# A four-layer graph network on one core: layer 3 in 34 shared tiles instead of 40, and a reordered passage from layer 1 to layer 2

## The reference

```python
# layer 2
Wh = h @ W
e = leaky_relu((Wh @ a1)[:, None] + (Wh @ a2)[None, :])
scores = where(adj > 0, e, -9e15)
x = x + elu(softmax(scores, axis=1) @ Wh)
# layer 3, for all pairs (i, j): a logarithmic map in the ball, masked, summed over j
u = mobius_add(-h_i, h_j);  un = clip(norm(u), 1e-7, 1 - 1e-5)
logs = 2 / lambda(h_i) * arctanh(un) * u / un
v_i = sum_j where(adj[i, j] > 0, logs[i, j], 0)
x = x + expmap(v, h)
```

## Time and profile before

| | |
|---|---|
| median of 3 runs | 1027.44 us (1025.52 to 1030.37) |
| the profiled execution's own time | 1028.51 us |
| its span in the trace | 1026.4 us (2.1 us lie around it) |
| busy share of the span | PE 89%, DVE 71%, ACT 55%, POOL 54% |
| chain that ended last | PE 73%, DVE 18%, issue 5%, ACT 3% |
| the layer 3 loop | 835.55 us to 994.57 us |
| passage from layer 1 to layer 2 | about 737 us to 762 us |

### The profile page before, as it was taken

The page is one execution under the profiler, slowest core; times in us unless marked ns, Lnnn a source line. Parts: engine busy times, 40 slices in busy tenths (PEclk is TensorE's granted clock), DMA queues, the critical chain, the costliest instruction groups (busy, mean ns, idle before and its releaser), DMA issues.

```text
span 1026.4 us, 17924 instructions
## 1 busy us (share of the span) xinstructions
PE 913.0 (89%) x6942; PEld 332.0 (32%) x6942; DVE 733.4 (71%) x1177; ACT 563.5 (55%) x977; POOL 556.2 (54%) x660
## 2 busy tenths in 40 slices
PE   6899999999999999999993798999769679999960
PEld 5733222222222222222232522333333244554420
DVE  4655568788888788887867477222549659999987
ACT  2688666666666666666650365001120248899960
POOL 2367569898898989898850000000000018899961
PEclk9689999999999999999995599999959867999985
DMA  8570211111112111110000000000000000000000
GB/s 173 139 141 17 62 61 38 59 40 64 40 32 65 35 70 40 60 38 26 23 12 0 1 1 1 1 1 2 1 1 1 1 0 1 1 0 1 1 0 21
DMA packets 22874, 32.62 MB, mean 32 GB/s; under 512 B 14427, under 2 KB 14555, under 8 KB 21766
## 3 DMA queue, kind: packets, MB, share of 16 engines
q1 hardware_dynamic: 20486, 23.10, 7.4%
q0 software_dynamic: 2304, 8.39, 4.4%
HBM read 38.58 MB, written 1.29 MB: 39 GB/s over the span
## 4 chain that ended last, share of the span: by engine, by line
PE 73%; DVE 18%; issue 5%; ACT 3%; SPq 0%; DMA 0%; POOL 0%; DVEq 0%; ACTq 0%
PE ps L1209 22%; PE ps L1219 11%; PE ps L1349 8%; PE ps L1196 6%; DVE big L453 5%; PE ps L1188 4%; PE ps L1374 3%; PE ps L1297 3%; PE ps L1410 2%; DVE big L785 2%; DVE big L450 2%; PE ps L1065 2%; PE ps L1287 2%; PE ps L1042 1%; PE ps L1382 1%
## 5 line engine op out<-in xcount | busy, mean ns | idle before, releaser
L587 DVE COPY_PREDICATED big<-mask,ps 128x512 f32<-128x512 uint8 x512 | 341.5, 729 | 113.6 <-PE ps L1196 109.9
L406 POOL TENSOR_SCALAR big<-big 128x512 f32<-128x512 f32 x512 | 355.7, 714 | 74.2 <-PE ps L1219 72.3
L933 ACT ACTIVATE ps<-ps 128x512 f32<-128x512 f32 x512 | 268.6, 583 | 141.6 <-PE ps L1188 141.3
L1209 PE MATMUL ps<-big 128*32 128x512 f32 x2048 | 253.6, 600 | 0.0
L422 POOL TENSOR_TENSOR big<-big 128x512 f32<-128x512 f32 x40 | 67.3, 1683 | 324.3 <-ACT big L1015 324.3
L1219 PE MATMUL ps<-big 128*32 128x512 f32 x1024 | 134.6, 597 | 0.0
L1188 PE MATMUL ps<-op_r,op_l 18*128 18x512 bf16 x512 | 111.7, 384 | 3.8 <-DVE big L587 2.2
L1209 PEld LDWEIGHTS ps<-big 128*32 128x32 f32 x2048 | 53.7, 109 | 119.7 <-issue 110.4
L1410 PE MATMUL ps<-big 66*128 66x512 f32 x160 | 86.2, 669 | 2.2 <-DVE big L758 1.3
L1196 PE MATMUL ps<-op_r,op_l 9*128 9x512 bf16 x512 | 74.7, 388 | 0.4 <-ACT ps L933 0.2
L453 DVE TENSOR_TENSOR big<-big,mask 128x512 f32<-128x512 f32 (+1 forms) x72 | 65.8, 933 | 12.7 <-ACT big L957 11.3
(11 more groups left out here) (258 smaller groups left out, 1153.9 us busy)
## 6 DMA issues: line engine op xcount, KB each, us to landing
big<-max_scratch SPq DMA_DIRECT2D x8, 1024.0 KB, 4.5
big<-rden_scratch SPq DMA_DIRECT2D x30, 256.0 KB, 3.3
big<-in_adj_dram POOLq DMA_DIRECT2D x12, 512.0 KB, 9.2
op_l<-split_scratch SPq DMA_DIRECT2D x56, 36.0 KB
op_r<-split_scratch SPq DMA_DIRECT2D x56, 36.0 KB
work<-in_adj_dram POOLq DMA_DIRECT2D x2, 512.0 KB, 12.9
h_nat<-in_adj_dram POOLq DMA_DIRECT2D x2, 512.0 KB, 11.8
x_nat<-in_x_dram SPq DMA_DIRECT2D x1, 512.0 KB, 5.1
```

What stands on the lines that cost most here:

```text
L406: pool.tensor_scalar(ring[:, k % RING, :], vrow[:, head % 2, i0:i0 + HALF], HUGE, g0[:, head, jt:jt + 1], ALU.min, ALU.max).then_inc(s["ba ...
L587: dve.copy_predicated(ring[:, k % RING, :], mask[:, jt, i0:i0 + HALF], ps[:, slot("tile", k), :])\
L933: act.activation(ps[:, at_slot, :], ps[:, at_slot, :], ACT.Relu, scale=-1.0).then_inc(s["relus"], 1)
L1209: m = pe.matmul(ps[32 * w:32 * (w + 1), MAIN, :], vp[:, head, jt + w // 2, 32 * (w % 2):32 * (w % 2 + 1)], ring[:, (u + w // 2) % RING, :] ...
```

## The change

It has two parts. In layer 3 a tile becomes a list of pieces. The strip on the diagonal of row `jt` keeps only the 128-blocks from the diagonal to the right (4, 3, 2 or 1 blocks for `jt % 4` = 0, 1, 2, 3), and short strips share a tile of 512 columns: 3 + 1 blocks of rows `jt-2` and `jt`, 2 + 2 blocks of rows `jt-4` and `jt`. All blocks off the diagonal are mirrored now, those inside the strips too, so all 34 tiles go through transposes and the mirror's mask product. Matmuls, the masked product and the mirror's mask product are issued once for each piece. In the passage from layer 1 to 2, PE's order is changed.

```diff
-        TILES3 = [(jt, c) for jt in range(NT) for c in range(jt // (HALF // P), BLOCKS)[::-1 if jt else 1]]
+        def diagonal(jt):
+            return (jt, jt // TB, jt % TB, TB)
+        TILES3 = [[diagonal(0)]] + [[(0, c, 0, TB)] for c in range(1, BLOCKS)]
+        for jt in range(1, NT):
+            TILES3 += [[(jt, c, 0, TB)] for c in range(BLOCKS - 1, jt // TB, -1)]
+            if jt % TB == 0:
+                TILES3.append([diagonal(jt)])
+            elif jt % TB == 3:
+                TILES3.append([diagonal(jt - 2), diagonal(jt)])
+            elif jt % (2 * TB) == TB + 2:
+                TILES3.append([diagonal(jt - TB), diagonal(jt)])
+        def pieces(k):
+            at = 0
+            for jt, c, b0, b1 in TILES3[k]:
+                yield at * P, jt, c, b0 * P, (b1 - b0) * P
+                at += b1 - b0
+        def mirrors(k):
+            for at, jt, c, i0, width in pieces(k):
+                skip = P if c == jt // TB else 0
+                if width > skip:
+                    yield at + skip, jt, c * TB + (i0 + skip) // P, (width - skip) // P
...
# DVE
-                if k >= LAG_M and MIRROR[k - LAG_M]:
+                if k >= LAG_M:
...
+                    dve.wait_ge(s["turned3"], m + 1)
+                    for at, jt, ib, blocks in mirrors(m):
+                        r = tt(wA[:, u, at:at + blocks * P].rearrange("p (j n) -> p j n", n=P),
+                               ps[:, 2, at:at + blocks * P].rearrange("p (j n) -> p j n", n=P),
+                               mask[:, ib:ib + blocks, jt * P:(jt + 1) * P], ALU.mult)
...
-                    tt(wC[:, u, :], wD[:, u, :], mask[:, jt, c * HALF:(c + 1) * HALF], ALU.mult).then_inc(s["wm3"], 1)
+                    for at, jt, c, i0, width in pieces(m):
+                        r = tt(wC[:, u, at:at + width], wD[:, u, at:at + width],
+                               mask[:, jt, c * HALF + i0:c * HALF + i0 + width], ALU.mult)
+                    r.then_inc(s["wm3"], 1)
...
# PE, layer 1 to 2
             turn_h(2)
             values2(1)
+            row_scores(0)
+            row_scores(1)
+            turn_h(3)
             values2(2)
-            for c in range(3):
-                row_scores(c)
-            turn_h(3)
             values2(3)
...
             pe.matmul(ps[:, 4, 3 * P - 1:3 * P], onesf[0:1, :], small[0:1, 20:21], start=True, stop=True).then_inc(s["mxb"], 1)
+            row_scores(2)
             row_scores(3)
...
# PE, layer 3: transposes and sums
+                    pe.wait_ge(s["wgt"], m + 1)
+                    if m >= 1:
+                        pe.wait_ge(s["mirrored"], m)
+                    for at, jt, ib, blocks in mirrors(m):
+                        for o in range(at, at + blocks * P, P):
+                            r = pe.transpose(ps[:, 2, o:o + P], wD[:, m % NW, o:o + P], ident[:, :])
...
+                    for n, (at, jt, c, i0, width) in enumerate(pieces(m)):
+                        pe.matmul(ps[0:DX, 4 + c, i0:i0 + width], h[:, jt, :], wC[:, u, at:at + width], start=(jt == 0),
+                                  stop=(FINAL[c] == (m, 0, n)))
+                    pe.wait_ge(s["mirrored"], m + 1)
```

More of the change, by code:

```diff
@@ L345, in gnn_stack @@
         n1 = len(TILES1)
-        TILES3 = [(jt, c) for jt in range(NT) for c in range(jt // (HALF // P), BLOCKS)[::-1 if jt else 1]]
-        n3 = len(TILES3)
-        MIRROR = [c > jt // (HALF // P) for jt, c in TILES3]
-        MIRRORS = [sum(MIRROR[:k + 1]) for k in range(n3)]
+        def diagonal(jt):
[9 more added lines that the diff above has]
+                TILES3.append([diagonal(jt - TB), diagonal(jt)])
+        n3 = len(TILES3)
+        def pieces(k):
[8 more added lines that the diff above has]
+                    yield at + skip, jt, c * TB + (i0 + skip) // P, (width - skip) // P
+        FINAL = {}
+        for k in range(n3):
+            for n, (at, jt, c, i0, width) in enumerate(pieces(k)):
+                FINAL[c] = (k, 0, n)
+            for n, (at, jt, ib, blocks) in enumerate(mirrors(k)):
+                FINAL[jt // TB] = (k, 1, n)
         LAG_T, LAG_M, LAG_S = 4, 5, 6
@@ L1409, in _ @@
                             pe.wait_ge(read, k)
-                        pe.matmul(ps[:, bank, :], lhs3[0:DX, jt * P:(jt + 1) * P], rhs[0:DX, c * HALF:(c + 1) * HALF],
-                                  start=True, stop=True).then_inc(sem, 1)
+                        for at, jt, c, i0, width in pieces(k):
+                            r = pe.matmul(ps[:, bank, at:at + width], lhs3[0:DX, jt * P:(jt + 1) * P],
+                                          rhs[0:DX, c * HALF + i0:c * HALF + i0 + width], start=True, stop=True)
+                        r.then_inc(sem, 1)
                 m = k - LAG_T
-                if 0 <= m < n3 and MIRROR[m]:
+                if 0 <= m < n3:
                     pe.wait_ge(s["wgt"], m + 1)
-                    if MIRRORS[m] > 1:
-                        pe.wait_ge(s["mirrored"], MIRRORS[m] - 1)
-                    for j in range(HALF // P):
-                        r = pe.transpose(ps[:, 2, j * P:(j + 1) * P], wD[:, m % NW, j * P:(j + 1) * P],
-                                         ident[:, :])
+                    if m >= 1:
[3 more added lines that the diff above has]
+                            r = pe.transpose(ps[:, 2, o:o + P], wD[:, m % NW, o:o + P], ident[:, :])
                     r.then_inc(s["turned3"], 1)
@@ L1422, in _ @@
                 if m >= 0:
-                    u, (jt, c) = m % NW, TILES3[m]
+                    u = m % NW
                     pe.wait_ge(s["wm3"], m + 1)
-                    r = pe.matmul(ps[0:DX, 4 + c, :], h[:, jt, :], wC[:, u, :], start=(jt == 0),
-                                  stop=(jt == (c + 1) * (HALF // P) - 1))
-                    if MIRROR[m]:
-                        pe.wait_ge(s["mirrored"], MIRRORS[m])
-                        for j in range(HALF // P):
-                            r = pe.matmul(ps[0:DX, 4 + jt * P // HALF, jt * P % HALF:jt * P % HALF + P],
-                                          h[:, c * (HALF // P) + j, :], wA[:, u, j * P:(j + 1) * P],
-                                          start=False, stop=False)
+                    for n, (at, jt, c, i0, width) in enumerate(pieces(m)):
+                        pe.matmul(ps[0:DX, 4 + c, i0:i0 + width], h[:, jt, :], wC[:, u, at:at + width], start=(jt == 0),
+                                  stop=(FINAL[c] == (m, 0, n)))
+                    pe.wait_ge(s["mirrored"], m + 1)
+                    for n, (at, jt, ib, blocks) in enumerate(mirrors(m)):
+                        for j in range(blocks):
+                            r = pe.matmul(ps[0:DX, 4 + jt // TB, jt % TB * P:jt % TB * P + P], h[:, ib + j, :],
+                                          wA[:, u, at + j * P:at + (j + 1) * P], start=False,
+                                          stop=(FINAL[jt // TB] == (m, 1, n) and j == blocks - 1))
                     r.then_inc(s["sums"], 1)
```

11 lines of the change are left out of this document (3 added, 8 removed).

## The result

The changed kernel takes 1011.33 us (median of 4 runs, 1009.67 to 1018.69) against 1026.48 us for the kernel before (4 runs, 1024.45 to 1030.37). The ratio is 0.9866, 95% interval 0.9837 to 0.9894: 1.3% faster. The ratio weighs all runs; the two medians alone would give 0.985, and the ratios further on weigh all runs in the same way. The forecast was 1009.0, in a range of 1000.5 to 1018.0.

A forecast was written before the change was run, and what follows sets the result against it. Layer 3 was taken as bound by DVE's turn and the DVE-POOL gate, both 3.6 to 3.7 us; the passage by PE. Passage -6.5 and layer 3 -12.0 take 1028.5 to 1010.0, less 1.1 to the median: 1009 us, range 1000.5 to 1018.

The forecast's parts named there:

- Step 1: Passage from layer 1 to 2: row products 0 and 1 ahead of the last transposes, 2 behind the maximum; -6.5 us.
- Step 2: Layer 3: 40 turns become 34; start +0.8 us, then 26 turns instead of 32 at 3.72 us, 96.7 us, less 0.6.
- Step 3: Layer 3, PE: fine on average, but whole tiles in a row make L779 lose the gate once; +1.3 us (0 to 2.6).
- Step 4: Layer 3: POOL enters between a split tile's two masked products, 1.4 us each, three tiles in the loop; +4.2 us.
- The rival without a stall: Split tiles in layer 3: DVE issues the second piece so tightly that POOL stays out; 1004 us, chance 0.20.
- Step 5: End of layer 3: 16 us from the last L785 to the end of the sums, +4.9 us; another +4 if the clock falls.
- Half clock or more lost gates: Layer 3: PE at half clock in the end, or more lost gates, +4 to +6 us; 1014 us, chance 0.20.
- The passage without gain: Passage from layer 1 to 2: ACT's table load or the row products become late, no gain; 1015.5 us, chance 0.04.
- the slower case: Layer 3: whole tiles in a row keep PE late, L779 loses to L426 nearly every turn; 1040 us, chance 0.03.

The follow-up runs named there:

- the kernel with every stall removed: Changed kernel with the six shared tiles' masks packed by ACT and ACT's exponential for tile k-2 moved ahead of tile k-1's exp and ln: 1006.20 us, ratio 0.9812.

## Why the prediction was right, and where it wasn't

**Step 1, the passage: right.** 6.5 us forecast, 6.6 in the trace, 6.5 alone in the time. The row products behind the maximum stayed hidden, as the comparison of PE's and ACT's start had it.

**Step 2, six turns fewer: right in the turn, short in the start.** The 20 turns of the loop without a stall average 3.70 us, so that 26 of them make 96.3 (96.1 forecast). But the start costs 2.15 us instead of 0.8. In the kernel before the clock rises 23.2 us after tile 0's L785, in the changed one 26.8, although transposes now begin one tile earlier. PE is at the half clock for 3.6 us longer, and DVE waits 2.60 us for it at 854.04. I had taken the clock's rise as fixed. The rise is at 26 to 27 us in all kernels with 34 tiles and at 23.2 in the one with only the passage changed, so it belongs to layer 3's part; what in PE's work moves it stays open.

**Step 3, PE: this step failed.** It said "on average PE is fine", since 127 us were less than the 134.5 of before. The comparison that counts is with DVE's time for the same turns: 127 / 34 = 3.74 us a turn against 3.70. And an average over all tiles is too kind, because part of the sums falls behind the last turn. In the 26 turns of the loop PE has 98.5 / 26 = 3.79 us a turn, as the kernel with every stall removed shows in 99.10 us. PE was short by 0.09 us a turn on average over the whole loop, not only in the first twelve tiles. (Before, 14 of the loop's 32 tiles had no mirror, more than the "every fourth tile or so" of the prediction, and PE was far from short.) Each time its lag reaches DVE's L481 the margin of 0.15 us is gone, L811 loses the gate, and 1.3 us are paid at once: three lost gates instead of one, +2.6 us.

The second slip is in what a lost gate gives back. The prediction had 1.1 us, enough for six turns of 0.17, so that one lost gate would do. But the traces have the next ones after four turns each (7, 11, 15). Timeline of PE over the first of these long turns, in the changed kernel:

```profile
860.75 1.88 PE L1446 MATMUL ps<-big 66*128 66x512 f32 x4
863.00 0.63 PE L1456 MATMUL ps<-ident,big 128*128 128x128 f32 x4 [0.37 <-DVE big L484]
...
865.20 1.88 PE L1446 MATMUL ps<-big 66*128 66x512 f32 x4
```

DVE's turn takes 5.01 us, but PE's takes 4.45 instead of 3.89, because its transposes wait for DVE's late mirror's mask product. So PE gains only 0.56 us, and in the fourth turn of 0.17 that is used up. A fourth gate would have been lost, had not the splits' stalls given PE its lead back: leaving out the masks of second pieces brought it out at turn 24.

**Step 4, the split masked products: right.** 1.4 us each forecast, 1.3 measured (5.01 against 3.70, and 1.32 in the kernel with all products split). The Trainium skill, "SBUF — State Buffer", section "Who interferes with whom", has the shared pair of ports as a lock for a whole instruction, taken in the order of issue. The traces agree: 1.83 us for two pieces with POOL waiting, 0.76 without. What a single row couldn't show and the split of all products does: between two instructions of DVE that follow each other directly, a waiting POOL gets in each time. The rival without a stall is refuted. One reading of the prediction was loose: L422 ends 1.13 us, not 1.27, behind the end of the masked product's record (871.07 against 869.94); counted from the product's start, as the gate's sum does, the 3.68 us stand.

**Step 5, the end: right in its size, with a wrong part.** 16 us forecast, 16.74 measured. The clock stayed at 1.00, as taken. The stall of tile 30 was foreseen, a second one was not: at 965.08 the masked product of tile 31, one instruction of 512 columns, loses against L457, issued 0.08 us earlier, and lasts 1.72 us. It is the same kind of loss by an 0.1 us margin.

Together: 1.35 at the start, 2.5 in the loop and 0.7 in the end are the 4.6 us by which layer 3 gave 7.4 instead of 12.0. Of these the loop's are shown by experiment (a kernel without lost gates and splits, one without splits), the start's only by the traces. The single profile hid them by starting layer 3 earlier for another reason.

**The rivals.** No stall at the split tiles (1004) is refuted. Half clock or more lost gates (1014) is half right: more gates were lost and the clock stayed up. With the start and the end they make up the 4.6 us of the traces, of which the medians show 3.3 (15.1 us gained, where the forecast had 18.4). The passage without gain and the slower case didn't come; the argument against the latter held in kind, a lost turn gives PE back what several turns use up, but four turns and not six.

**What beats it.** Packing the six masks brings the ratio to 0.983, with ACT's order also moved to 0.981 (of these two, the second is shown over the first by the trace alone: the medians are 1006.26 and 1006.20 us). Of a change that merges short pieces of work, that is the part that should have come with it: the pieces share a tile for every engine, but not for the one instruction that stands at the gate.

## What to carry to other kernels

Where instructions of two engines exclude each other, as DVE's with both inputs in SBUF and POOL's do here, count how many enter, not only how many elements they handle: one instruction split in two cost 1.3 us here against 0.07 of work, because the other engine was already waiting. When several engines are within 3% of one another, compare each one's total with the total of the engine that sets the pace, over the same turns, and not with its own total before; a shortage of 0.09 us a turn was paid in steps of 1.3 us. And when a profile's difference agrees with a sum, look first whether the unchanged code ahead of the change stands at the same time in both.

## What was unexpected of the hardware

- A late release can be better than an early one. Holding POOL's L457 back by 0.5 us removed the lost gates of turns 7, 11 and 15; with packed masks no gate was lost from tile 7 on, and it took the loop from 101.55 to 99.10 us.
- The granted clock stayed at 0.50 for 23 to 27 us of a PE that was busy without a gap (10.00 of 10 us), and rose 3.6 us later in the changed kernel, whose transposes begin a tile earlier. In the kernel with all products split, where PE stood idle in between (busy for 0.07 of the 1 us from 23 us on), it rose only 33 us after tile 0's L785. But in the two kernels with DVE's order changed PE was idle for short times too, and the rise came at 26 to 27 us all the same. No run here separates what moves it.
- An idle gap of 2.51 us in the end brought the clock from 1.00 to 0.50 in one kernel, one of 2.38 us did not in another. In the kernel before PE had gaps of 2.29 and 1.21 us, and the last sums ran at the half clock; the changed kernel had gaps of 2.38 and 1.89 us with more work in and behind them, and its sums ran at the full one. What decides isn't shown.
